# Where the operands of the split-fp32 matmuls begin in SBUF

## The reference

```
h  = layernorm(x)
q  = h @ Wq;  k = ctx @ Wk;  v = ctx @ Wv            # 8 heads of 64
x  = x + softmax(q k^T / 8) v @ Wo + bo
h  = layernorm(x) * gamma + beta
y  = silu(h @ dequant(fc1_q) + fc1_bias)             # 256 -> 1024
z  = y @ dequant(fc2_q) + fc2_bias                   # 1024 -> 256
out = x2 + 0.5 z   (x2 = x + h, since the block has a residual of its own inside)
```

## The kernel before

| stage | weights (bytes past a multiple of 512) | moving operand |
|---|---|---|
| FC1 | w1: 192 | hT: 128 |
| FC2 | y: 128 | w2: 192 |
| AO | pT: 352 | vw: 448 |
| S | xT: 160 | m: sixteen starts, among them 0, 16, 32, 96, 112, 128, 192, ... 432, since a half is 308 columns (1232 bytes) |

## Time and profile before

### The profile page before, as it was taken

How to read it: one execution, slowest core, us unless ns; L and a number is a source line. 1 busy time by engine, 2 the same in 40 slices (tenths; PEclk the granted TensorE clock), 3 DMA queues, 4 the chain that set the end, 5 groups by cost and what they waited for, 6 DMA issues and landing times.

```text
span 195.8 us, 3879 instructions
## 1 busy us (share of the span) xinstructions
PE 186.8 (95%) x1502; PEld 180.5 (92%) x1502; DVE 122.9 (63%) x262; ACT 122.0 (62%) x227; POOL 116.3 (59%) x159
## 2 busy tenths in 40 slices
PE   6999899899899999999999999999999998998994
PEld 6889699699899999999999999999999998997894
DVE  0297987999788375945495459545964677531332
ACT  3158880699647962797079728783679435763480
POOL 5033997289975974397619770987169734477020
PEclk9999999999999999999999999999999999999999
DMA  5996991000001000000000000000010001000101
GB/s 148 293 394 186 301 366 34 2 0 3 2 0 54 3 0 0 30 27 0 3 27 27 3 0 28 30 2 0 13 44 0 3 0 54 3 0 0 54 3 54
DMA packets 9480, 10.72 MB, mean 55 GB/s; under 512 B 2268, under 2 KB 8183, under 8 KB 9335
## 3 DMA queue, kind: packets, MB, share of 16 engines
q1 hardware_dynamic: 8837, 9.70, 15.3%
q10 hardware_dynamic: 626, 0.79, 1.4%
HBM read 8.38 MB, written 2.10 MB: 54 GB/s over the span
## 4 chain that ended last, share of the span: by engine, by line
PE 68%; DVE 18%; DMA 4%; POOL 4%; issue 4%; ACT 1%; SPq 0%
PE H L798 19%; PE S L765 13%; PE T L786 13%; PE T L810 11%; DMA wv_sb<-in_L_xattn_Wv 4%; PE S L772 4%; DVE hT_lo L576 4%; DVE smax L527 3%; DVE w_lo L594 2%; DVE hT_hi L574 2%; PE S L719 2%; PE T L749 2%; DVE x_sb L583 1%; POOL y_lo L286 1%; POOL probs L254 1%
## 5 line engine op out<-in xcount | busy, mean ns | idle before, releaser
L286 POOL TENSOR_TENSOR y_lo<-y,y_hi 128x512 fp32r<-128x512 f32 x28 | 37.8, 1364 | 5.1 <-ACT y_hi L400 4.5
L254 POOL TENSOR_TENSOR probs<-probs,rsum 128x616 f32<-128x616 f32 x16 | 19.2, 1220 | 34.3 <-DVE rsum L546 34.3
L798 PE MATMUL H<-hT_hi,w_hi 128*128 128x256 f32 x128 | 37.0, 289 | 1.7 <-issue 0.8
L810 PE MATMUL T<-w_hi,y_hi 128*128 128x256 f32 x128 | 37.0, 289 | 1.3 <-POOL y_lo L286 0.8
L798 PE MATMUL H<-hT_hi,w_lo 128*128 128x256 f32 x128 | 35.8, 279 | 0.0
L798 PE MATMUL H<-hT_lo,w_hi 128*128 128x256 f32 x128 | 35.8, 279 | 0.0
L810 PE MATMUL T<-w_hi,y_lo 128*128 128x256 f32 x128 | 35.6, 278 | 0.0
L810 PE MATMUL T<-w_lo,y_hi 128*128 128x256 f32 x128 | 35.6, 278 | 0.0
L396 ACT ACTIVATE y<-H,vec 128x256 f32<-128x256 f32 x64 | 26.6, 469 | 10.7 <-PE H L798 10.7
L369 ACT ACTIVATE probs<-probs,rstd 128x616 f32<-128x616 f32 x16 | 12.9, 807 | 27.4 <-DVE probs L534 27.4
L798 PEld LDWEIGHTS H<-hT_hi,w_hi 128*128 128x128 f32 x128 | 24.1, 189 | 3.3 <-DVE hT_lo L576 2.1
(11 more groups left out here) (119 smaller groups left out, 457.0 us busy)
## 6 DMA issues: line engine op xcount, KB each, us to landing
q_sb<-in_L_ffn_fc_q SPq DMA_DIRECT2D x2, 1024.0 KB, 8.7
out_x<-x_sb SPq DMA_DIRECT2D x16, 128.0 KB, 1.7
x_sb<-in_x SPq DMA_DIRECT2D x7, 256.0 KB, 8.3
s_sb<-in_L_ffn_fc_scales SPq DMA_DIRECT2D x2, 512.0 KB, 12.6
s_sb<-in_L_ffn_fc_scales SPq DMA_DIRECT2D x1, 1024.0 KB, 7.9
wq_sb<-in_L_xattn_Wq SPq DMA_DIRECT2D x1, 512.0 KB, 6.7
wo_sb<-in_L_xattn_Wo SPq DMA_DIRECT2D x1, 512.0 KB, 9.4
wk_sb<-in_L_xattn_Wk ACTq DMA_DIRECT2D x1, 384.0 KB, 5.2
```

The source lines that it names most:

```text
L254: nc.gpsimd.tensor_tensor(p, p, rsum[:, j, :].unsqueeze(2).to_broadcast([P, HEADS, J]), ALU.mult).then_inc(norm_done, 1)
L286: nc.gpsimd.tensor_tensor(y_lo[:, two, :], y[:, two, :], f32(y_hi[:, two, :]), ALU.subtract).then_inc(y_lo_done, 1)
L798: ins = mm(r[:, q * W:(q + 1) * W], wt[:, c, m * P:(m + 1) * P], ht[:, c, :], start=i == 0, stop=i == len(steps) - 1)
L810: ins = mm(o, yt[:, m, j * P:(j + 1) * P], wt[:, m, :], start=m == 0 and i == 0, stop=m == M - 1 and i == 2)
```

## The change

All SBUF tensors are declared in another order. First x_sb and the big tensors whose size is a multiple of 512 bytes, among them the weights of the fp32r matmuls (w1, xT, pT); then a filler of 256 bytes; then the moving operands (w2, m, vw, hT); then a filler of another 256 bytes; then the small tensors, whose sizes are added up so that a last filler ends them at a multiple of 512; then, as before, the early buffers and y_hi and y_lo over them. The result is that all weights begin 128 bytes past a multiple of 512, and all moving operands 384 past one.

For M this needs the halves to be a multiple of 512 bytes apart: 384 columns instead of 308, of which 308 are used. So the axes of half and head no longer merge: `m_heads` has one dimension more, and VectorE's m_lo is written by two instructions of half the size in each of the 8 calls. ScalarE's m_hi stays one instruction. Nothing else changes: the same matmuls, waits and order.

```diff
+LINE = 512
+SKEW = 256
+GRAIN = 32
+    HALF_COLS = -(-HALF * 4 // LINE) * LINE // 4
+        def small(name, shape):
+            nonlocal used
+            used += -(-math.prod(shape[1:]) * 4 // GRAIN) * GRAIN
+            return sb(name, shape)
         x_sb = sb("x_sb", [P, NT, D])
...
         w1_hi, w1_lo = sb("w1_hi", [P, C, F], F32R), sb("w1_lo", [P, C, F], F32R)
+        xT_hi, xT_lo = sb("xT_hi", [P, C, W], F32R), sb("xT_lo", [P, C, W], F32R)
+        pT_hi, pT_lo = sb("pT_hi", [P, UT, JC, P], F32R), sb("pT_lo", [P, UT, JC, P], F32R)
...
+        sb("skew", [P, SKEW // 4])
         w2_hi, w2_lo = sb("w2_hi", [P, M, D], F32R), sb("w2_lo", [P, M, D], F32R)
-        m_hi, m_lo = sb("m_hi", [P, B, C, 2, HALF], F32R), sb("m_lo", [P, B, C, 2, HALF], F32R)
+        m_hi, m_lo = sb("m_hi", [P, B, C, 2, HALF_COLS], F32R), sb("m_lo", [P, B, C, 2, HALF_COLS], F32R)
         vw_hi, vw_lo = sb("vw_hi", [P, B * JC, D], F32R), sb("vw_lo", [P, B * JC, D], F32R)
         hT_hi, hT_lo = sb("hT_hi", [P, C, W], F32R), sb("hT_lo", [P, C, W], F32R)
+        sb("skew_end", [P, (LINE - SKEW) // 4])
...
+        sb("rest_of_line", [P, (-used % LINE) // 4])
...
-            return m[:, b, n // 2, :, :].rearrange("p h (k e j) -> p (h k) e j", k=K // 2, e=2)[:, :, n % 2, :]
+            return m[:, b, n // 2, :, 0:HALF].rearrange("p h (k e j) -> p h k e j", k=K // 2, e=2)[:, :, :, n % 2, :]
...
-                    nc.vector.scalar_tensor_tensor(m_heads(m_lo, b, n), ps[bank][:, 0:HALF].rearrange("p (k j) -> p k j", k=K), DH ** -0.5 / D,
-                                                   f32(m_heads(m_hi, b, n)), ALU.mult, ALU.subtract).then_inc(freed[bank], 1)
+                    r = ps[bank][:, 0:HALF].rearrange("p (h k j) -> p h k j", h=2, k=K // 2)
+                    for h in range(2):
+                        ins = nc.vector.scalar_tensor_tensor(m_heads(m_lo, b, n)[:, h, :, :], r[:, h, :, :], DH ** -0.5 / D,
+                                                             f32(m_heads(m_hi, b, n)[:, h, :, :]), ALU.mult, ALU.subtract)
+                    ins.then_inc(freed[bank], 1)
...
-                            ins = mm(o, xt[:, c, j * P:(j + 1) * P], m[:, b, c, h, :], start=n == 0, stop=n == len(steps) - 1)
+                            ins = mm(o, xt[:, c, j * P:(j + 1) * P], m[:, b, c, h, 0:HALF], start=n == 0, stop=n == len(steps) - 1)
```

More of the change, by code:

```diff
@@ L1 @@
+import math
 from contextlib import ExitStack
@@ L80, in sem @@
             return stack.enter_context(nc.semaphore(name))
-        x_sb = sb("x_sb", [P, NT, D])
[L83 to L87, removed]
+        used = 0
+        def small(name, shape):
+            nonlocal used
+            used += -(-math.prod(shape[1:]) * 4 // GRAIN) * GRAIN
+            return sb(name, shape)
+        x_sb = sb("x_sb", [P, NT, D])
         q1_sb = sb("q1_sb", [P, C, F], I32)
@@ L93, in build_program @@
         w1_hi, w1_lo = sb("w1_hi", [P, C, F], F32R), sb("w1_lo", [P, C, F], F32R)
+        xT_hi, xT_lo = sb("xT_hi", [P, C, W], F32R), sb("xT_lo", [P, C, W], F32R)
+        pT_hi, pT_lo = sb("pT_hi", [P, UT, JC, P], F32R), sb("pT_lo", [P, UT, JC, P], F32R)
+        hT = sb("hT", [P, C, W])
+        hn = sb("hn", [P, UT, D])
+        y = sb("y", [P, M, W])
+        probs = sb("probs", [P, UT, JC * P])
+        ident = sb("ident", [P, P])
+        bo_sb = sb("bo_sb", [1, D])
+        bo_hi, bo_lo = sb("bo_hi", [1, D], F32R), sb("bo_lo", [1, D], F32R)
@@ L94, in build_program @@
+        b2_half = sb("b2_half", [P, D])
+        sb("skew", [P, SKEW // 4])
         w2_hi, w2_lo = sb("w2_hi", [P, M, D], F32R), sb("w2_lo", [P, M, D], F32R)
-        m_hi, m_lo = sb("m_hi", [P, B, C, 2, HALF], F32R), sb("m_lo", [P, B, C, 2, HALF], F32R)
+        m_hi, m_lo = sb("m_hi", [P, B, C, 2, HALF_COLS], F32R), sb("m_lo", [P, B, C, 2, HALF_COLS], F32R)
         vw_hi, vw_lo = sb("vw_hi", [P, B * JC, D], F32R), sb("vw_lo", [P, B * JC, D], F32R)
-        ident = sb("ident", [P, P])
-        neg_half = sb("neg_half", [P, NT])
@@ L100, in build_program @@
[L100 to L113, removed]
-        hT_hi, hT_lo = sb("hT_hi", [P, C, W], F32R), sb("hT_lo", [P, C, W], F32R)
-        y = sb("y", [P, M, W])
+        hT_hi, hT_lo = sb("hT_hi", [P, C, W], F32R), sb("hT_lo", [P, C, W], F32R)
@@ new lines, in build_program @@
+        sb("skew_end", [P, (LINE - SKEW) // 4])
+        vec = small("vec", [P, 2 * C + M])
+        gamma_sb, beta_sb, b1_sb = vec[:, 0:C], vec[:, C:2 * C], vec[:, 2 * C:2 * C + M]
+        neg_half = small("neg_half", [P, NT])
+        table_probe = small("table_probe", [P, 1])
+        bn1, mv1 = small("bn1", [P, NT, 6]), small("mv1", [P, NT, 2])
+        veps1, rstd1 = small("veps1", [P, NT]), small("rstd1", [P, NT])
+        smax, ssum, rsum = small("smax", [P, UT, HEADS]), small("ssum", [P, UT, HEADS]), small("rsum", [P, UT, HEADS])
@@ L119, in build_program @@
+        bn2, mv2 = small("bn2", [P, 2, UT, 6]), small("mv2", [P, 2, UT, 2])
+        vars2, rstd2 = small("vars2", [P, 2, 2, UT]), small("rstd2", [P, 2, 2, UT])
+        neg_rstd2, res_scale, res_shift = small("neg_rstd2", [P, 2, UT]), small("res_scale", [P, 2, UT]), small("res_shift", [P, 2, UT])
+        sb("rest_of_line", [P, (-used % LINE) // 4])
         early = ExitStack()
@@ L351, in m_hi_part @@
                     r = wait_filled(act, f"M{b}.{n}")
-                    nc.scalar.activation(m_heads(m_hi, b, n), r[:, 0:HALF].rearrange("p (k j) -> p k j", k=K), ACT.Copy,
+                    nc.scalar.activation(m_heads(m_hi, b, n), r[:, 0:HALF].rearrange("p (h k j) -> p h k j", h=2, k=K // 2), ACT.Copy,
                                          scale=DH ** -0.5 / D).then_inc(m_hi_done, 1)
```

## The result

The changed kernel's median is 199.04 us against 197.69 us, ratio 1.007 with a 95% interval of 1.0047 to 1.0093. Both are medians of five runs; of the five of the changed kernel one took 260.15 us at a mean granted clock of 0.66 and is left out of the ratio. The forecast was 195.7 us, the range ended at 198.7. What came is the rival I had given 0.18: the new relation locks FC on AO's level (199.1 us by its own sum). The profiled span went from 195.8 to 197.2 us.

A forecast was written before the change was run, and what follows sets the result against it. The prediction took TensorE, busy 95% of the span, as the bound, its fp32r matmuls losing time. From 197.65 us: AO -1.28, S -0.75, FC 0, m_lo +0.1 gave 195.7 us; range 191.6 to 198.7.

The forecast's parts named there:

- the rival I had given 0.18: All FC stages, above all the last 96 matmuls, locked at AO's 119.3 ns, AO and S unchanged: 199.1 us; chance 0.18.
- all starts become multiples of 64 in common, as in FC: Address assumption for AO and S: weights no longer 32 bytes past a multiple of 64, so FC's matmul speeds apply.
- FC: forecast 0: 366 FC1 and FC2 matmuls on the path keep their mixture, 192 at 117.7 ns and 174 at 113.2: 0 us.
- My bound for it, +1.37: Slow-side bound of the FC term: all 366 matmuls at AO's 119.3 ns, +1.37 us.
- AO: forecast -1.28 us: 210 AO matmuls on the path go from 119.3 to 113.2 ns each, saving 1.28 us.
- S: forecast -0.75 us: 108 S matmuls of 308 columns on the path go from 141.8 to 134.9 ns each, saving 0.75 us.
- m_lo: forecast +0.1: Splitting VectorE's m_lo into 16 half-size instructions adds 0.1 us on the path, at batch 0's first S.
- S's chance pair at 256 apart: In S, batch 1's m_hi at 416 against xT at 160 gained nothing; read as against 256 bytes being a cure by itself.
- The three levels: Fixed losses of fp32r matmuls: 5, 10 or 12 ns beyond 108 for 256 columns, steps of 113.2, 117.7 and 119.3 ns.
- the last 96: FC matmuls at the kernel's end, already at the low level, 5.45 us for 48; over 11.3 us would show the prediction wrong.
- the waits that cap the gain: First FC1 half and second S tile wait for other engines; without these waits the low level would be worth nearly twice.
- addresses don't matter: Rival: timing alone sets the matmul levels, so only m_lo's +0.1 us is left: 197.8 us; chance 0.22.

The follow-up runs named there:

- Experiment 2: Matmul streams alone, weights starting at byte 32, 256 moving columns at every 16-byte offset: loss about 32 cycles at difference 0 or 256, 16 at 192.
- experiment 9: Streams alone: 308 columns every 8 bytes lost 28 to 44 cycles; 256 columns at difference 192, entered behind 1 to 12 transposes, lost 16.0 ten times, 26.7 twice.
- Experiment 3: Kernel before with only the edit of M (halves 384 columns apart, m_lo in two instructions, a filler): 197.46 us, ratio 1.000.
- 11: Changed kernel with w2 and hT 192 bytes past their weights, vw and m left at 256: 197.5 us, ratio to before 1.0004.
- 12: Kernel before with four fillers only, putting w2 and vw at 192 modulo 256 from their weights: 196.63 us, ratio 0.9955.
- experiment 10: Changed kernel with w2, vw and hT 192 bytes past their weights and m at the weights' own start: 195.6 us, ratio to before 0.9903.
- experiment 1: Matmul streams alone, weights at byte 0, 256 moving columns at every 16-byte offset: 120.0 ns a step at difference 0 or 256, 113.3 at 192.
- Experiment 8: Streams alone with 32, 64 or 128 weight columns and 128 to 512 moving ones, at differences 0, 64, 192: 128 beside 128 took 111.7 ns a step.
- experiment 6: Changed kernel with all moving operands 192 bytes past their weights instead of 256: 196.0 us, ratio to before 0.993.

## Why the prediction was wrong

**The step that failed is the reading of the addresses.** I wrote that what counts is that "all starts become multiples of 64 in common, as in FC", put AO and S on FC's low level and left FC's mixture alone. Experiment 2 shows that multiples of 64 don't matter. What counts is the relation modulo 256. Read so, the kernel before had FC1 at 192, the best there is, FC2 at 64 (mostly 26.7, at times 16) and AO at 96 (32, the worst level of the grid of 16 bytes): its fastest stages were no accident of timing alone. The change took FC from there to 0, where every stage loses 32. I had forecast 0 for FC and -2.03 us for AO and S; the runs showed +1.5 and about 0. The terms, by the mean steps of the two traces:
- FC: forecast 0. 366 matmuls from 115.6 (192 at 117.7, 174 at 113.2) to 119.8 ns: +1.55 us. My bound for it, +1.37, was a little small, as it took AO's level at 119.3 rather than 120.0.
- AO: forecast -1.28 us. 119.8 to 119.9 ns: 0. Its relation went from 96 to 0, from one loss of 32 to another.
- S: forecast -0.75 us. 12 matmuls in seven pairs by 0.9 ns less, -0.08; but pair 0's stage took 147 ns a step, the level of 44 that experiment 9 also met: +0.12. Together about 0. That the low level carries over to 308 columns was false as well: no relation tried gives them under 28 cycles, 140 ns. And S had stages there already: pair 1's ran at 140.1 ns in the kernel before, so "never show a stage at the lower level" misread it.
- m_lo: forecast +0.1. Experiment 3 shows 0 within 0.15%, 0.3 us, for m_lo together with a slightly faster S, and the first S did not start later.

The sum is +1.6 us; the spans differ by 1.4. That the rival's 199.1 came within 0.1 us is in part luck: its FC term was 0.2 too small, and the 0.1 of m_lo in it did not come. The bookkeeping of what lies on the path was sound.

**What I weighed wrongly.** S's chance pair at 256 apart gained nothing, and I used that only against a full cure, not as a sign that 256 is bad. It was weak evidence either way, since 308 columns behave otherwise than 256. FC1 and FC2 I took as one relation, 64 apart, without the sign; one is +64, the other -64. A table of level against signed relation, stage by stage, would have shown that both kinds reach 113 and AO at +96 never does.

**What was right.** The three levels and what each is worth; that the moment of entry chooses between levels (experiments 3, 9, 11 and 12); that the last 96 could only lose; the waits that cap the gain. In the rows on the waits of TensorE's weight load, the time it waits for hT_lo was 2.1 us in six waits before and 2.0 in the changed kernel; in experiment 10, with faster stages ahead, it is the first row here:

```profile
PEld H L817 <- DVE hT_lo L595: 2.5, 6, 0.6
```

**The pages.** The rule cited in the prediction, from "SBUF — State Buffer", "Who interferes with whom" in the Trainium skill, by which the moving operand and the weights have ports of their own and TensorE waits for nobody, is not borne out here: with no other compute engine at work the step is 113.3 or 120.0 ns by the relation alone (experiment 1). Its consequence was my rival "addresses don't matter", 197.8 us, and the measurement decides against it.

**What stays open.** What the two streams share, and why a loss has these levels. Experiment 8 rules out one turn for each 16 bytes of weights; no run isolates a cause. Nor did I find a layout or entry that holds the low level surely: experiment 10 left its last 96 matmuls at 117.8 ns, some 0.4 us.

## What to carry to other kernels

In a TensorE-bound stream of fp32r matmuls with 128 weight columns and 256 moving ones, lay the moving operand 192 bytes past its weights modulo 256, not 0 and not 256: in this kernel the difference between the two was 3 us of 199. Measure the distance between starts of neighbouring matmuls, stage by stage, and set it against the signed difference of the operands' addresses before moving anything; and sweep that difference, for the shape at hand, with a small kernel of streams alone (with 64 weight columns beside 256 moving ones, or with 308 or 512 moving ones beside 128, 0 was better than 192), as one run of 250 us answered what the full kernel's trace left ambiguous. An edit that moves one operand also moves the entry of the next stage, so the gain is to be measured whole.

## What the runs showed of the hardware that I had not expected

- The relation counts modulo 256 bytes, and it is not smooth: for 256 columns 16 cycles at 192, 32 at 196; 24 at 12, 48 at 8.
- A stage at 113.3 ns holds its place in absolute time. In the trace of before, the mean starts of FC1's low stages, taken modulo 6.67 ns (16 cycles), lie at 1.3 to 1.7 ns in all of them from 64 to 187 us, those of FC2's at 3.0 to 3.3; single starts are known to 1 ns. In the trace of experiment 6 all 30 low stages, FC1, AO and FC2 alike, have one place. No run shows why. Steps of 272 and 288 cycles are multiples of 16, and three of 282.67 are 848, 53 times 16.
- A weight load of 128 fp32r columns sets a pace of its own, 111.7 ns a matmul beside 128 moving columns, at each of three relations (experiment 8).
